# Softmax sums moved from SBUF to SBUF, reciprocals spread by two matmuls, and the output projection in two chunks

## The reference, cut to what matters

```python
h = tok(x, scharr)                               # (32, 256, 256)
h = concatenate([broadcast(cls_tok), h], axis=1) # (32, 257, 256)
def attn(x):                                     # T = 257, C = 256, H = 16, hd = 16
    q, k, v = split(x @ w_qkv + b_qkv)
    att = softmax(where(causal, q @ k.T / sqrt(hd), -inf))
    y = (att @ v).transpose(0, 2, 1, 3).reshape(B, T, C)
    return y @ w_out + b_out
h = h + attn(layernorm(h))
h = h + ffn(layernorm(h))                        # fake-quantised gate, up and down weights
```

## Time and profile before

| | us |
|---|---|
| median of 3 runs | 1469.43 |
| profiled execution, its own time | 1472.33 |
| its span, first to last instruction | 1470.6 |
| PE busy | 1096.2 |
| DVE busy | 933.9 |
| ACT busy | 660.3 |
| POOL busy | 508.6 |

### The profile page before, as it was taken

How to read it: one execution, slowest core, us unless ns; L and a number is a source line. 1 busy time by engine, 2 the same in 40 slices (tenths; PEclk the granted TensorE clock), 3 DMA queues, 4 the chain that set the end, 5 groups by cost and what they waited for, 6 DMA issues and landing times. The chain is left out here.

```text
span 1470.6 us, 28592 instructions
## 1 busy us (share of the span) xinstructions
PE 1096.2 (75%) x9702; PEld 749.7 (51%) x9702; DVE 933.9 (64%) x1955; ACT 660.3 (45%) x1107; POOL 508.6 (35%) x549
## 2 busy tenths in 40 slices
PE   2458888888878888888888788888766476755666
PEld 1236665665656666666656656666654233322332
DVE  1234666666666667565665765676647588888764
ACT  1235554454554444444444544554322476743332
POOL 5324444344454444444443443453320000002332
PEclk9978999999999898899989998999976699996655
DMA  3655454444554444454445545342420133411664
GB/s 88 164 128 129 123 133 113 126 132 120 139 145 111 125 125 124 118 144 126 120 115 121 136 117 142 102 111 75 125 56 16 39 140 135 176 60 35 201 235 151
DMA packets 157011, 177.21 MB, mean 121 GB/s; under 512 B 27897, under 2 KB 147614, under 8 KB 153886
## 3 DMA queue, kind: packets, MB, share of 16 engines
q1 hardware_dynamic: 156958, 176.52, 43.8%
HBM read 90.30 MB, written 35.16 MB: 85 GB/s over the span
## 5 line engine op out<-in xcount | busy, mean ns | idle before, releaser
L509 ACT ACTIVATE prob<-ST 128x772 f32<-128x772 f32 x256 | 209.1, 817 | 351.4 <-PE ST L883 347.4
L668 DVE TENSOR_REDUCE mneg<-SX 128x2 f32<-128x258 f32 x256 | 106.6, 416 | 203.5 <-PE SX L869 203.4
L866 PE MATMUL SX<-kst,qst 96*128 96x257 bf16 (+1 forms) x1024 | 169.0, 260 | 87.9 <-DMA qst<-qpart 48.8
L670 DVE TENSOR_REDUCE mneg<-SX 128x2 f32<-128x514 f32 x256 | 173.5, 678 | 0.0
L866 PEld LDWEIGHTS SX<-kst,qst 96*128 96x128 bf16 x1024 | 98.1, 103 | 144.6 <-issue 75.6
L883 PE MATMUL ST<-qst,kst 98*128 98x256 bf16 (+2 forms) x1536 | 149.2, 233 | 28.9 <-DMA qst<-mpart 28.0
L883 PEld LDWEIGHTS ST<-qst,kst 98*128 98x128 bf16 x1536 | 127.3, 104 | 52.0 <-DMA qst<-mpart 22.8
L869 PE MATMUL SX<-mask_s,ident_b 128*128 128x256 bf16 x512 | 148.5, 290 | 0.0
L444 POOL TENSOR_SCALAR_AFFINE_SELECT prob<-prob 128x1016 f32<-128x1016 f32 x128 | 144.9, 1132 | 0.0
L985 PE MATMUL M<-wo_pad,yn 128*128 128x256 f32 x512 | 139.0, 419 | 0.8 <-DVE yn L741 0.8
L900 PE MATMUL G<-prob,vaug 128*32 128x256 f32 (+2 forms) x3072 | 125.1, 295 | 4.6 <-POOL prob L444 4.6
(11 more groups left out here) (220 smaller groups left out, 2011.5 us busy)
## 6 DMA issues: line engine op xcount, KB each, us to landing
kst<-kpart SPq DMA_DIRECT2D x192, 128.5 KB, 2.5
gst<-gray_dram SPq DMA_DIRECT2D x96, 256.0 KB
qst<-qpart SPq DMA_DIRECT2D x192, 128.0 KB, 2.4
yn<-rec_dram SPq DMA_DIRECT2D x128, 128.0 KB, 3.9
h_dram<-hb SPq DMA_DIRECT2D x12, 1280.0 KB, 4.6
hb<-h_dram SPq DMA_DIRECT2D x12, 1280.0 KB, 6.1
wg_raw<-in_x SPq DMA_DIRECT2D x48, 256.0 KB, 3.7
wu_raw<-in_x SPq DMA_DIRECT2D x48, 256.0 KB, 4.2
```

Source lines behind the costliest of these rows:

```text
L509: nc.scalar.activation(prob[:, g % 2, 2 * (u % 2):2 * (u % 2) + 2, 0:QEND], ST[:, :, 0:QEND], ACT.Exp).then_inc(exp_done, 1)
L668: nc.vector.tensor_reduce(mneg[:, 0, 2 * u:2 * u + 2], SX[:, :, S0:S0 + P + 1], AX.X, ALU.max, negate=True)
L670: nc.vector.tensor_reduce(mneg[:, 1, 2 * u:2 * u + 2], SX[:, :, S1:S1 + T], AX.X, ALU.max, negate=True).then_inc(max_done, 1)
L866: mm(SX[:, r, at:at + k], qst[par][0:SR, 2 * u + r, P * t:P * t + P], kst[par][0:SR, 2 * u + r, 0:k], start=t == 1, stop=False)
```

## The change

The four sums of a 32-row block are moved from `yun` straight into 4 rows of a 16x256 tile `den` (SBUF to SBUF, four DMAs), and DVE takes the reciprocal there. Two matmuls against 0/1 columns of the constant table (`spread_rec`) copy each reciprocal onto the 16 rows of its head, in bank 1 of `G`. Four further SBUF to SBUF moves pack groups 1 and 3 of `yun` onto the partitions 32j+16 to 32j+31 of groups 0 and 2 (over the sums, once these have been moved). DVE then multiplies 128x512 instead of 128x1024, after `maxima(1)` instead of after `maxima(2)`, and the projection takes two matmuls per half instead of four, against `wop`. The bias `b_out` moves into the first layer norm's copy to `h2`, which becomes an addition on DVE. `den_dram`, `rec_dram` and the moves through them go. The weight `wop` is loaded by eight DMAs in place of `wo_pad`'s four and one, with one constant load more and one fill of POOL less.

```diff
+    for j in range(4):
+        for g in range(4):
+            first = C_SEL + P * (g // 2) + 32 * j + HD * (g % 2)
+            c[4 * j + g, first:first + HD] = 1.0
...
-        wo_pad = sb("wo_pad", [P, 4, D])
+        wop = sb("wop", [P, KC, D])
+        bo_row = sb("bo_row", [P, D])
...
-        yn = sb("yn", [P, 4, IMG])
-        den = sb("den", [P, 4 * 4 * IMG // P])
+        yn = sb("yn", [P, KC, IMG])
+        den = sb("den", [H, IMG])
...
-                first = P * (j % 2) + HD * (j // 2)
-                sp.dma_start(wo_pad[32 * j:32 * j + HD, :, :],
-                             w_out.rearrange("(c g e d) n -> c e d g n", c=KC, g=4, e=2)[j % 2, j // 2]
-                             ).then_inc(s_wo, 16)
-
-            sp.dma_start(wo_pad[HD:HD + 1, 0, :], b_out.rearrange("(o n) -> o n", o=1)).then_inc(s_wo, 16)
+                for e in range(2):
+                    at = 32 * j + HD * e
+                    sp.dma_start(wop[at:at + HD, :, :],
+                                 w_out.rearrange("(a c e b d) n -> a b e d c n", a=2, c=KC, e=2, b=2)[j % 2, j // 2, e]
+                                 ).then_inc(s_wo, 16)
...
-                if valid(bO):
-                    wait(sp, rec_done, bO, 1, 1)
-                    sp.dma_start(spread(rec_dram), den[:, :]).then_inc(rec_saved, 16)
                 if valid(n + 1):
                     wait(sp, gray_step, bW, 2, 2)
                     load_x(n + 1, odd)
-                if valid(bO):
-                    wait(sp, out_done, bO - 1, 1, 1)
-                    wait(sp, rec_saved, bO, 16, 16)
-                    for j in range(4):
-                        sp.dma_start(yn[32 * j:32 * j + 32, :, :], rec_dram[j:j + 1].broadcast_to([32, 4, IMG])
-                                     ).then_inc(rden_loaded, 16)
...
                 if valid(bT):
                     wait(sp, yun_ready, bT, 2, 2)
                     for j in range(4):
-                        sp.dma_start(den_dram[j:j + 1], yun[32 * j + HD:32 * j + HD + 1, :, :]
-                                     ).then_inc(den_saved, 16)
+                        sp.dma_start(den[4 * j:4 * j + 4, :], yun[32 * j + HD:32 * j + HD + 1, :, :]
+                                     ).then_inc(den_moved, 16)
 
                 def query_rows(slots):
                     if valid(bP):
...
                 wait(sp, q_low, bP, 1, 1)
                 query_rows(range(0, 3))
                 if valid(bT):
-                    wait(sp, rec_saved, bT - 1, 16, 16)
-                    wait(sp, den_saved, bT, 64, 64)
-                    sp.dma_start(den[:, :], spread(den_dram)).then_inc(den_loaded, 16)
+                    wait(sp, den_moved, bT, 64, 64)
+                    for j in range(4):
+                        sp.dma_start(yun[32 * j + HD:32 * j + 2 * HD, 0:4:2, :], yun[32 * j:32 * j + HD, 1:4:2, :]
+                                     ).then_inc(y_moved, 16)
                 query_rows(range(3, 6))
...
+            bo2 = bo_row[:, :].rearrange("p (o d) -> p o d", o=1).broadcast_to([P, QT, D])
+
+            def stats(b, rows, s, st, ag, ve, free, bias=None):
...
+                if bias is not None:
+                    nc.vector.tensor_tensor(h2[:, rows2(b), :], rows[:, :, :], bias, ALU.add)
+                else:
+                    nc.vector.tensor_scalar(h2[:, rows2(b), :], rows[:, :, :], 1.0, None, ALU.mult)
...
-                    wait(dve, den_loaded, bO, 16, 16)
+                    wait(dve, den_moved, bO, 64, 64)
                     nc.vector.reciprocal(den[:, :], den[:, :]).then_inc(rec_done, 1)
...
                 maxima(bS, 1)
+                if valid(bO):
+                    wait(dve, rec_spread, bO, 1, 1)
+                    wait(dve, y_moved, bO, 64, 64)
+                    wait(dve, out_done, bO - 1, 1, 1)
+                    nc.vector.tensor_tensor(yn[:, :, :], yun[:, 0:4:2, :],
+                                            G[:, 1, :].rearrange("p (c t) -> p c t", c=KC), ALU.mult
+                                            ).then_inc(yn_done, 1)
                 maxima(bS, 2)
-                if valid(bO):
-                    wait(dve, rden_loaded, bO, 64, 64)
-                    nc.vector.tensor_tensor(yn[:, :, :], yun[:, :, :], yn[:, :, :], ALU.mult).then_inc(yn_done, 1)
...
+                        if g == 2:
+                            wait(pe, yn_done, b - 1, 1, 1)
...
+                def spread_rec():
+                    if valid(bO):
+                        wait(pe, rec_done, bO, 1, 1)
+                        wait(pe, yun_ready, bO, 2, 2)
+                        for c in range(KC):
+                            last = mm(G[:, 1, IMG * c:IMG * c + IMG], tab[0:H, C_SEL + P * c:C_SEL + P * c + P],
+                                      den[:, :], start=True, stop=True)
+                        last.then_inc(rec_spread, 1)
...
-                        for g in range(4):
-                            last = mm(M[0][:, D * t:D * t + D], yn[:, g, P * t:P * t + P], wo_pad[:, g, :],
-                                      start=g == 0, stop=g == 3)
+                        for c in range(KC):
+                            last = mm(M[0][:, D * t:D * t + D], yn[:, c, P * t:P * t + P], wop[:, c, :],
+                                      start=c == 0, stop=c == KC - 1)
...
                 scores_t(bT, odd, 4)
+                spread_rec()
                 outputs(bT, odd, 1)
```

More of the change, by code:

```diff
@@ L39 @@
 NB = B * IMG // TB
-C_ID, C_MS, C_BAND = 0, P, 2 * P
+C_ID, C_MS, C_SEL = 0, P, 2 * P
+C_BAND = C_SEL + 2 * P
 C_END = C_BAND + 3 * GR
@@ L74, in vit_tower @@
     gray_dram = nc.dram_tensor("gray_dram", [IMG + 2, IMG + 2], fp32, kind="Internal").ap()
-    den_dram = nc.dram_tensor("den_dram", [4, 4, IMG], fp32, kind="Internal").ap()
-    rec_dram = nc.dram_tensor("rec_dram", [4, 4, IMG], fp32, kind="Internal").ap()
     ctx = ExitStack()
@@ L212, in vit_tower @@
         yun_ready = sem("yun_ready")
-        den_saved, den_loaded = sem("den_saved"), sem("den_loaded")
-        rec_done, rec_saved = sem("rec_done"), sem("rec_saved")
-        rden_loaded = sem("rden_loaded")
+        den_moved, y_moved = sem("den_moved"), sem("y_moved")
+        rec_done, rec_spread = sem("rec_done"), sem("rec_spread")
         yn_done = sem("yn_done")
@@ L270, in vit_tower @@
         FIN = B + LAST - 1
-        N_CONST, N_WO, N_INIT = 24, 7, 5 + 2 * (2 + KT - 1)
+        N_CONST, N_WO, N_INIT = 25, 10, 4 + 2 * (2 + KT - 1)
         block = attention.enter_context(nc.Block())
@@ L294, in _ @@
                     const(taps[3 * GR + 2 * dx:3 * GR + 2 * dx + 2, f, :], tap.broadcast_to([2, 3]), slow=True)
+            const(bo_row[:, :], b_out.rearrange("(o n) -> o n", o=1).broadcast_to([P, D]))
             const(crow[:, 0, :], cls_tok[0, :, :])
@@ L325, in _ @@
             load_x(0, 0)
-            def spread(dram):
-                return dram.rearrange("j g t -> (j g t)").rearrange("(p f) -> p f", p=P)
             def max_rows(b, par, half_):
@@ L424, in _ @@
             fill(half[:, :], -0.5)
-            fill(wo_pad[:, :, :], 0.0)
             fill(one[:, :], 1.0)
@@ L681, in split @@
                     nc.vector.tensor_tensor(lo, M[1][0:H // 2, 0:IMG], hi, ALU.subtract).then_inc(msplit, 1)
-            def stats(b, rows, s, st, ag, ve, free):
+            bo2 = bo_row[:, :].rearrange("p (o d) -> p o d", o=1).broadcast_to([P, QT, D])
+            def stats(b, rows, s, st, ag, ve, free, bias=None):
                 wait(dve, s, b, LN, 1)
@@ L688, in stats @@
                 wait(dve, s, b, LN, 3)
-                nc.vector.tensor_scalar(h2[:, rows2(b), :], rows[:, :, :], 1.0, None, ALU.mult)
+                if bias is not None:
+                    nc.vector.tensor_tensor(h2[:, rows2(b), :], rows[:, :, :], bias, ALU.add)
+                else:
+                    nc.vector.tensor_scalar(h2[:, rows2(b), :], rows[:, :, :], 1.0, None, ALU.mult)
                 for t in range(QT):
@@ L749, in step @@
                                             ).then_inc(ln1, 1)
-                    stats(bC, edge, ln1, st1, ag1, ve1, lambda: wait(dve, rs1_done, bC - 1, 1, 1))
+                    stats(bC, edge, ln1, st1, ag1, ve1, lambda: wait(dve, rs1_done, bC - 1, 1, 1), bo2)
                 split(bS, 0)
```

## The result

The changed kernel takes **1609.84 us** (median of 4 runs, 1608.07 to 1618.01) against 1468.93 us before: a ratio of 1.098, interval 1.093 to 1.103, so 141 us slower. Slower was forecast, but at 1544 us and with 1578 as the upper end of the range. The profiled execution took 1611.07 us.

A forecast was written before the change was run, and what follows sets the result against it. A loop through `scores(0)` to `scores(3)` on PE, DVE to `split(0)`, SP's queue and landing sets the pace; 99 - 45 + 22 - 3 - 4 + 6 = +75 on 1472.3 gives 1547, less 2.9: 1544 us, range 1465 to 1578.

The forecast's parts named there:

- SP's queue: On SP, sum and packing moves issue at 0.643 us each ahead of the last query moves: +99 us, -3 for projection slack.
- `maxima(3)`: On DVE, the multiplication no longer waits for reciprocals ahead of `maxima(3)`, so it comes on time: -45 us.
- DVE's chain: On DVE from `maxima(3)` to `split(0)`: the bias addition counted at 0, with +7 us kept for the range.
- outside the steps: On PE, the shorter projection is on the path in the last two steps, which move no queries: -4 us.
- rivals of cheap issues, the first rival: On SP, SBUF to SBUF moves aren't dear as such, packing moves issue at 0.415 us: +10, 1479 us; chance 0.17.
- a queue that doesn't decide: At the wait of `scores(0)`, landing decides, not SP's queue length; only gains stay: -30, 1439 us; chance 0.13.
- the third rival: SP must also wait for the sums to land, 0.6 us a step, moves issue at 0.668: +111, 1580 us; chance 0.10.
- the lower bound: On SP, packing moves at the broadcast loads' 0.415 us: +1.24 us a step; with sums at 0, +37 us in all.
- Spreading matmuls: On PE between `scores_t(4)` and `outputs(1)`, two fp32 matmuls at 0.25 us full clock, 0.52 half: +22 us.
- Clock: On PE, a longer idle before `scores(0)` leaves later work at a lower clock: +6 us, between 0 and +22.

The follow-up runs named there:

- late: The change with only its SP queue reordered: sum moves after all six query moves, packing moves in the next step behind the maxima rows; 1436.58 us.
- den1: The change with the four sum moves merged into one DMA of the same 16 KB, at the same place in SP's queue; 1544.09 us.
- multlate: The kernel before with only its multiplication moved on DVE from ahead of `maxima(3)` to behind `split(0)`; 1458.16 us.
- warm20: The change with 20 bf16 matmuls of 256 columns that do no work added behind `turn_max(1)`, in PE's idle; 1546.26 us.
- best4: The change with merged sum move, reordered queue, first layer norm work behind `split(0)` and `maxima(4)`, and `project(1)` ahead of the maxima rows' wait; 1377.99 us.

## Why the prediction was wrong in size

The steps can be followed through the whole run, 31 of them from the first `scores(0)` (82.34 before, 80.67 after) to the last (1067.68 and 1206.57). Together they grow by 140.6 us, and what lies outside them shrinks by 1.9. Against the terms of the sum:

| us in all | forecast | measured |
|---|---|---|
| SP's queue | 99 - 3 | +101.5 |
| `maxima(3)` | -45 | -46.0 |
| PE, `scores(0)` to the end of `scores(3)` | 22 + 6 | +60.5 |
| DVE's chain | 0 | +24.6 |
| outside the steps | -4 | -1.9 |
| span | +75 | +138.7 |

**SP's queue, +99 us: right.** From one of the new moves to the next it is (611.21 - 608.54) / 4 = 0.67 us and (615.87 - 613.23) / 4 = 0.66, where the key moves' 0.643 was taken; a single issue lasts 0.599 and 0.621 us. The part of the step grew by 3.45 us. The rivals of cheap issues and of a queue that doesn't decide fell, the first by the rows of L374 and L388, the second by late and den1. The wait for the sums' landing, the third rival, costs nothing: 613.23 follows 613.12. One reading was wrong: moves with DRAM on one side don't end at 0.415 us, the reload itself takes 0.52 in the earlier trace rows. Only the lower bound and the first rival hang on it.

**`maxima(3)`, -45 us: right** in size, -1.63 us a step. But I took it for free, and it brought the larger part of what DVE's chain lost (below).

**Spreading matmuls, +22 us: too small.** I took 1.97 / 8 us from the earlier trace rows for one matmul. The eight are four matmuls of the program: each fp32 matmul leaves two records, and two of weight loads. The part of this document on the change shows it already, four and four matmuls of `project` on PE against 16 records a step (512 over 32). The right price is 0.53 us at full clock and about twice that at half: 1.06 us a step instead of 0.77, some 31 us in all.

**Clock, +6 us: far too small.** The work alone would have taken 10.59 us; it took 13.83. The slow clock costs 3.24 us a step, where it cost 11.80 - 9.53 = 2.27 before: +0.97, about 28 us over 29 steps, in place of 6. I bounded this by the slowest stretch that the kernel before showed, 12.7 us. The change has stretches of 17.5 us at 0.58, which the kernel before never had: a bound from old rows held only for the old pattern of idles. I also took the idle for 1.44 + 3.3 + 2 = 6.7 us in every step. It averages 4.2, and so PE's wait came to 136.9 us and not to 150 or more: between `split(0)` and the idle PE takes 17.55 - 4.23 = 13.3 us, where it took 14.11 - 1.18 = 12.9, and not the 2 us less that the shorter projection was to give.

**DVE's chain, 0: wrong**, +0.80 us a step, 24.6 us in all, and the largest single miss. 0.24 us are the addition, which takes 1.00 us and not the 0.69 of the earlier trace rows; it was kept for the range only. The other 0.56 have nothing to do with it: with `maxima(3)` on time, DVE comes to its 128x2 operation while POOL is at its subtraction, as it does in multlate, which has nothing else of the change. In the step that I read as undisturbed that operation was over at 571.38, 0.1 us before POOL began.

So the mechanism was right: SP's queue sets the step, and its issues cost what was said. The steps of the prediction that failed are three terms beside it, on the same loop: DVE's chain counted at nothing (24.6 us), the clock counted at 6 us (about 28), and the spreading matmuls priced by their records (22 for some 31). The forecast of 1544 us was 66 us low. The added cost of the clock goes with the idle that SP's queue makes (warm20), and most of DVE's with the lateness that the change removes (multlate): both are effects of the two terms that I had right.

## What to carry to other kernels

If a queue of DMAs stands ahead of what opens the next step, count its issues and not its bytes: put what isn't needed for that behind it, and merge small moves. A wait that two late things share hides the price of each; when one is removed, look for what it covered. An operation that comes on time may meet another engine's that it used to miss: look at what runs beside its new place. And an idle on PE that grows by some microseconds was paid twice here, once as idle and once as lower clock in the steps after; matmuls that do nothing can be worth their place there.

## What the runs showed of the hardware beyond what I expected

- The issue of a move from SBUF to SBUF takes 0.6 us on SP, whether it carries 4 KB (0.599), 16 KB (0.609), 32 KB (0.621) or 128 KB (0.607).
- An fp32 matmul of 256 columns takes 1.97 / 4 = 0.49 us at full clock, a bf16 one of as many columns 2.35 / 20 = 0.12 (warm20, from the row below): 4.2 times as long, under two records.

```profile
586.00 2.35 PE L1052 MATMUL SX<-mask_s,ident_b 128*128 128x256 bf16 x20
```

- The reciprocal of 256 elements a partition takes 1.73 us against 0.34 for 32: about 6.2 ns for each element more. It was hidden.
- A 128x2 operation of DVE takes 0.17 us alone and 0.58 to 1.07 when POOL is in a subtraction of 128x512, and ends with it.
- 20 matmuls that do no work took 64 us off the change, 6 of them 50 us off best4, and 10 in the kernel before 0.6%.
